# Attention scores by key differences for half of the key pairs, in a convolution and attention kernel on one core

## The reference

```python
B, C, H, W = x.shape                      # 2, 64, 96, 96
h = group_norm1(x, n1_g, n1_b)
f = dwconv(h, w3, b3) + dwconv(h, w5, b5) + dwconv(h, w7, b7)
g = jax.nn.sigmoid(conv1x1(f, gate_w, gate_b))
x = x + conv1x1(f * g, proj_w, proj_b)
h = group_norm1(x, n2_g, n2_b)
N = H * W                                 # 9216
q = conv1x1(h, q_w, q_b).reshape(B, C, N).transpose(0, 2, 1)
k = conv1x1(h, k_w, k_b).reshape(B, C, N)
v = conv1x1(h, v_w, v_b).reshape(B, C, N).transpose(0, 2, 1)
attn = jax.nn.softmax(jnp.einsum('bnc,bcm->bnm', q, k) * C ** -0.5, axis=-1)
out = jnp.einsum('bnm,bmc->bnc', attn, v)
return x + out.transpose(0, 2, 1).reshape(B, C, H, W)
```

## Time and profile before

| | |
|---|---|
| median of 3 runs | 2752.18 us (2750.35 to 2754.17) |
| the profiled execution | 2755.12 us, of which the profile's span is 2753.1 us |
| granted TensorE clock, mean over the span | 0.995 of 2.4 GHz |
| busy share of the span | PE 96%, POOL 83%, ACT 80%, DVE 68%, weight loads 41% |
| accumulating DMAs into accD | 612 of 512 KB, 4.9 us from issue to landing |
| the chain of work that ended last | 83% of it on PE |

### The profile page before, as it was taken

How to read it: one execution, slowest core, us unless ns; L and a number is a source line. 1 busy time by engine, 2 the same in 40 slices (tenths; PEclk the granted TensorE clock), 3 DMA queues, 4 the chain that set the end, 5 groups by cost and what they waited for, 6 DMA issues and landing times.

```text
span 2753.1 us, 87253 instructions
## 1 busy us (share of the span) xinstructions
PE 2650.6 (96%) x36712; PEld 1124.0 (41%) x36712; DVE 1859.0 (68%) x1942; ACT 2193.4 (80%) x2216; POOL 2298.6 (83%) x2088
## 2 busy tenths in 40 slices
PE   7889999999999999999988999999999999999998
PEld 4243344444444444444433344444444444444443
DVE  5576666767676766766557666667667666666664
ACT  4467788888888888888866788888888888888887
POOL 1356999988999898999964799999999899999987
PEclk9999999999999999999999999999999999999999
DMA  6138888877878777777601687787777777777771
GB/s 205 45 78 184 165 167 168 164 160 161 168 163 166 161 163 162 163 163 161 134 8 37 141 165 162 158 169 159 163 163 161 160 163 163 161 162 163 162 157 30
DMA packets 138706, 406.85 MB, mean 148 GB/s; under 512 B 19272, under 2 KB 45384, under 8 KB 137808
## 3 DMA queue, kind: packets, MB, share of 16 engines
q0 software_dynamic: 102816, 356.56, 64.3%
q1 hardware_dynamic: 35504, 44.75, 6.0%
HBM read 16.41 MB, written 9.44 MB: 9 GB/s over the span
## 4 chain that ended last, share of the span: by engine, by line
PE 83%; DVE 8%; issue 3%; POOL 2%; ACT 2%; DMA 1%; SPq 0%; ACTq 0%; POOLq 0%; DVEq 0%
PE ps L1053 36%; PE ps L1042 32%; PE ps L1062 9%; DVE mxp L838 5%; POOL arena L493 2%; PE ps L1187 2%; DVE ot L888 2%; ACT arena L597 1%; PE ps L1102 1%; DVE pvc L875 1%; DMA accD<-arena 1%; PE ps L1215 1%; ACT ps L633 1%; PE ps L1090 1%; PE ps L1230 0%
## 5 line engine op out<-in xcount | busy, mean ns | idle before, releaser
L838 DVE TENSOR_REDUCE mxp<-ps 128x1 f32<-128x1024 f32 x1296 | 1581.6, 1224 | 742.7 <-PE ps L1062 742.6
L493 POOL TENSOR_TENSOR arena<-arena 128x512 f32<-128x512 f32 x1224 | 1746.2, 1427 | 184.2 <-ACT arena L597 99.3
L597 ACT ACTIVATE arena<-ps,bnd 128x1024 f32<-128x1024 f32 x1296 | 1373.7, 1111 | 340.2 <-PE ps L1042 317.4
L1053 PE MATMUL ps<-arena,vals 64*64 64x512 f32 x10368 | 1243.2, 591 | 6.6 <-DVE pvc L875 6.6
L1042 PE MATMUL ps<-arena 64*64 64x512 f16 x15552 | 1064.7, 376 | 10.6 <-ACT ps L633 7.3
L633 ACT ACTIVATE ps<-arena 128x1024 f32<-128x1024 f16 x612 | 628.7, 1027 | 54.2 <-ACT arena L597 1.5
L1042 PEld LDWEIGHTS ps<-arena 64*64 64x64 f16 x15552 | 456.5, 106 | 432.1 <-issue 152.3
L1062 PE MATMUL ps<-arena,QM 64*64 64x512 f16 x5184 | 514.5, 385 | 37.5 <-DVE mxp L838 32.5
L1053 PEld LDWEIGHTS ps<-arena,vals 64*64 64x64 f32 x10368 | 368.8, 133 | 408.2 <-issue 319.3
L510 POOL DMA_DIRECT2D accD<-arena x544 | 488.6, 898 | 13.2 <-DMA accD<-arena 9.9
L1062 PEld LDWEIGHTS ps<-arena,QM 64*64 64x64 f16 x5184 | 150.4, 103 | 547.1 <-DVE mxp L838 480.1
(11 more groups left out here) (127 smaller groups left out, 707.2 us busy)
## 6 DMA issues: line engine op xcount, KB each, us to landing
accD<-arena POOLq DMA_DIRECT2D x612, 512.0 KB, 4.9
accD<-accD POOLq DMA_DIRECT2D x34, 512.0 KB, 7.1
arena<-accD POOLq DMA_DIRECT2D x68, 256.0 KB, 5.2
arena<-arena SPq DMA_DIRECT2D x144, 64.0 KB, 2.5
arena<-in_x_rows SPq DMA_DIRECT2D x8, 816.0 KB, 9.8
xs<-in_x SPq DMA_DIRECT2D x4, 1152.0 KB, 16.0
f_scratch<-arena SPq DMA_DIRECT2D x32, 144.0 KB
f<-f_scratch SPq DMA_DIRECT2D x16, 288.0 KB, 10.6
```

Of the source, the lines that this page charges most:

```text
L493: nc.gpsimd.tensor_tensor(accA[:, n % 2, :], accA[:, n % 2, :], e, ALU.add).then_inc(adda_free, 1)
L597: nc.scalar.activation(E[:, :, slot_of(n % 2, p), :], ps[:, S_BANK + 2 * buf:S_BANK + 2 * buf + 2, :], ACT.Exp, scale=bnd[:, 6:7]).then_in ...
L838: nc.vector.reduce_max(flat(mxp[:])[:, v:v + 1], flat(ps[:, bank:bank + 2, :]), AX.X).then_inc(mx_free, 1)
L1053: a = nc.tensor.matmul(ps[C * t:C * t + C, ACC_BANK + r, :], V[rows, p, t, :], E[rows, t, slot_of(par, p), :], start=(p == 0), stop=(p == ...
```

## The change

Keys of a chunk of 512 are now split: for pairs with p % 4 of 2 or 3, the key matrix holds the difference to the keys of the pair two before (`KD` its high part, the second half of KL its low part). Their matmuls add onto the scores that already stand in the buffer, so such a pair has neither a seed nor the `one16` product: 12 matmuls, and the maximum is already subtracted. Pairs with p % 4 of 0 or 1 are seeded, both, from pair 4 on. In blocks other than the first of an image, pair 24 is not seeded (the row sums of the block before use its banks), and pairs 0 and 1 never are. E has 10 slots instead of 12. GpSimd adds two pairs at a time (128 x 1024). ScalarE copies both banks of weighted values (128 x 1024) and a DMA folds them; VectorE's `add_pv` goes. GpSimd adds the output's two terms (`finish`) after ScalarE added a bias to one of them (`add_bias`); VectorE's `write_out` goes from the blocks. The next block's maxima are placed before the last exponential of a block instead of after it, by 16 matmuls instead of 8. SP loads the second image's x and convolved values in pieces over the first image's blocks.

```diff
-NSLOT = 12
+NSLOT = 10
...
-        def is_seeded(b, p):
-
-            return b in SEEDED and p % 2 == 1 and p >= 3
+        def by_difference(p):
+
+            return p % GP >= 2
+
+        def is_seeded(j, p):
+
+            return p >= GP and not by_difference(p) and not (j and p == RESTART)
...
-                nc.gpsimd.tensor_tensor(accA[:, n % 2, :], accA[:, n % 2, :], e, ALU.add).then_inc(adda_free, 1)
+                at = slot_of(n, 2 * g)
+                pool.wait_ge(e_ready, NPAIR * n + 2 * g + 3)
+                pool.wait_ge(adda_free, NSLOT + NPAIR * n + 2 * g)
+                nc.gpsimd.tensor_tensor(accA[:, n % 2, :], accA[:, n % 2, :], E[:, 0, at:at + 2, :].rearrange("p s c -> p (s c)"),
+                                        ALU.add).then_inc(adda_free, 2)
...
+                def keys_and_difference(c, chunk):
+
+                    n = 2 * NCH * b + c
+                    cols = slice(chunk * CH, chunk * CH + DIFF)
+                    pool.wait_ge(t_ready, n + 1)
+                    pool.wait_ge(hi_ready, n + 1)
+                    nc.gpsimd.tensor_tensor(T[:, c % 4, DIFF:CH], T[:, c % 4, DIFF:CH], T[:, c % 4, 0:DIFF], ALU.subtract
+                                            ).then_inc(diff_ready, 1)
+                    nc.gpsimd.tensor_tensor(KL[:, cols], T[:, c % 4, 0:DIFF], KH[:, cols], ALU.subtract)
...
-                nc.scalar.activation(flat(pvc[:]), ps[:, ACC_BANK, :], ACT.Copy).then_inc(acc_copied, 1)
+                nc.scalar.activation(pvc.rearrange("p r h c -> p r (h c)"), ps[:, ACC_BANK:ACC_BANK + 2, :], ACT.Copy
+                                     ).then_inc(acc_copied, 1)
+
+            def add_bias(b, j):
+
+                done = (b * (NBLK // 2) + j // 2) * 32
+                act.wait_ge(xst_ready[j % 2], done + 32)
+                nc.scalar.activation(xst[:, j % 2, :], xst[:, j % 2, :], ACT.Identity, bias=prm[:, VB:VB + 1]
+                                     ).then_inc(xst_biased, 1)
...
                 for p in range(NPAIR):
+                    if p == NPAIR - 1 and j + 1 < NBLK:
+                        place_maxima(n + 1)
                     exponentials(n, p)
-                    if p == ROW_SUMS + 3 and j:
+                    if p == RESTART - 1 and j:
                         copy_row_sums(n - 1, S_BANK)
-                    if p + 2 < NPAIR and is_seeded(b, p + 2):
+                    if p + 2 < NPAIR and is_seeded(j, p + 2):
                         seed(b, j, p + 2)
                     if p == 1 and j:
                         move_pv(n - 1)
+                    if p == RESTART + 2 and j:
+                        add_bias(b, j - 1)
...
-                terms = ((KH[:, keys], 0), (KL[:, keys], 0), (KH[:, keys], 1), (one16[:], 2))
-                if seeds is not None:
-                    pe.wait_ge(seeded, seeds)
+                if is_seeded(j, p):
+                    pe.wait_ge(seeded, seeds_before(b, j, p + 1))
+                keys = slice(p * P, (p + 1) * P)
+                of_hi, hi = KH, keys
+                if by_difference(p):
+                    at = p // GP * DIFF + p % 2 * P
+                    of_hi, hi = KD, slice(at, at + P)
+                terms = ((of_hi[:, hi], 0), (KL[:, keys], 0), (of_hi[:, hi], 1), (one16[:], 2))
+                opens = not by_difference(p) and not is_seeded(j, p)
+                if not opens:
                     terms = terms[:3]
```

More of the change, by code:

```diff
@@ L437, in _ @@
                 if b + 1 < B:
-                    load_x(b + 1)
+                    load_x_chunk(b + 1, 0)
                     sp.wait_ge(v_ps, NCH * (b + 1))
[L440 to L444, removed]
+                    for i in range(1, NCH - 1):
+                        attend(b, i, 0, True)
+                        load_x_chunk(b + 1, i)
+                        attend(b, i, 1, True)
+                        get_convolved(b + 1, (i - 1) // 2, ((i - 1) % 2,))
+                else:
+                    with sp.Fori(1, NCH - 1) as ii:
+                        for par in (0, 1):
+                            attend(b, ii, par, True)
                 attend(b, NCH - 1, 0, True, max_queries=False)
+                if b + 1 < B:
+                    load_x_chunk(b + 1, NCH - 1)
+                    get_convolved(b + 1, NSET - 1, (1,))
                 attend(b, NCH - 1, 1, True, queries=False, max_queries=False)
@@ L712, in _ @@
                         n = 2 * NCH * b + i
+                        before = ITEMS[i - 1]
                         by, plus = bnd[:, 4 + which:5 + which], bnd[:, 7 + which:8 + which]
@@ L720, in _ @@
                                              bias=plus, scale=by).then_inc(t_ready, 1)
+                        if i and before[0] == 1:
+                            act.wait_ge(diff_ready, NCH * b + before[1] + 1)
+                            nc.scalar.activation(KD[:, before[1] * DIFF:(before[1] + 1) * DIFF], T[:, (i - 1) % 4, DIFF:CH], ACT.Copy
+                                                 ).then_inc(dh_ready, 1)
                 place_maxima(blk(b, 0))
@@ L1124, in visit, with following @@
                         max_scores(par, v // NCH, v % NCH, NVIS * (n + 2) + v)
+                def following(p):
+                    q = p + 2
+                    if q < NPAIR:
+                        if q == RESTART and not first:
+                            pe.wait_ge(rs_copied, n)
+                        scores(b, j, q, n0 + p + 1)
+                    elif looks:
+                        if q == NPAIR:
+                            pe.wait_ge(m_ready, n + 2)
+                            pe.wait_ge(qs_in[1 - par], staged)
+                        scores(b, j + 1, q - NPAIR, n0 + p + 1)
+                if looks:
+                    pe.wait_ge(qm_in[1 - par], max_staged)
                 for p in range(0, NPAIR, 2):
-                    if p == 0 and looks:
-                        pe.wait_ge(qm_in[1 - par], max_staged)
                     if p == NPAIR - AHEAD and looks == 2:
```

246 lines of the change are left out of this document (140 added, 106 removed).

## The result

The changed kernel takes 2930.18 us (median of 4 executions, 2927.93 to 2930.86), the kernel before 2752.22 (also of 4, 2750.35 to 2754.17): ratio 1.0645, 95% interval 1.0627 to 1.0664. It is 6.5% slower. The profiled execution took 2930.86 us, with a span of 2929.1.

A forecast was written before the change was run, and what follows sets the result against it. TensorE was taken to set the pace, with ScalarE's seeds nearly as long a path. 2755.1 + 223 (36 blocks at +6.2) - 9.5 (loads) + 5 (prologue) = 2973.6, forecast as 2970 us, 7.9% slower; range 2900 to 3040.

The forecast's parts named there:

- The closed loop: TensorE's scores wait for ScalarE's second seed, delaying the next difference scores: four pairs take 8.29 instead of 7.34 us.
- Seed to seed, 2.25: ScalarE, from seed p+2's start to seed p+3's, one exponential between: 2.25 us, from 3.26 less 1.01.
- The rest of a block, 10.5 - 1.4: A block's two iterations outside the eight groups, 10.5 us before, change by -1.4 in sum.
- the maxima's spread, +0.2: 16 small matmuls instead of 8 when maxima are spread: +0.2 us a block, bounds 0 and 0.4.
- The loads' -9.5: Spreading the second image's loads saves the second block's extra 9.5 us.
- VectorE's two lines: Output write L888 and sum L875 leave the chain: 1.5 us a block saved, bounds 0 and 2.5.
- The prologues: More GpSimd operations and a further ScalarE copy in the prologue, mostly under VectorE's reductions: +5 us, from 0 to +20.
- Waits at scores p+3: TensorE idle before the second seeded pair's scores, 1.2 to 1.5 us, eight or so a block, some 400 us in all.
- A: Rival: faster, the second seed does not hold TensorE (wait under about 0.6 us a group); 2670 or 2570 us; 7%.
- B: Rival: much slower, TensorE's clock falls after each standstill, 430 us more, 3400 us; 3%.
- C: Rival: slower still, a dear wide GpSimd sum makes exponentials wait for slots; 3080 us, from 3050 to 3120; 7%.
- D: Rival: seed delays and TensorE's saving cancel, at a wait near 0.6 us; 2%.

The follow-up runs named there:

- experiment 5: Changed kernel with seeds at p % 4 = 3 and 0, the even pair weighed between the scores in most iterations, `add_bias` two pairs later: 2726.58 us.
- experiment 2: Changed kernel with the even pair's weighing and second look-ahead between the two scores in iterations whose pairs are both seeded: 2671.90 us, 0.9707 of the kernel before.
- experiment 8: Changed kernel with an unread 256-element ScalarE copy in front of the first seed of a group (p % 4 = 2), 7 a block forecast: 2951.81 us.

## Why the prediction was right, and where its sizes were off

**The closed loop** is shown. Its length follows TensorE's part of it (2.79 and 1.72 us, in experiment 5, give 8.22 and 7.14) and ScalarE's (0.10 and 0.30 more give 8.32 and 8.52), and ScalarE's work outside it costs nothing. The changed kernel itself has a third length of TensorE's part: in the last block of an image no look-aheads stand in it, it is 2.36, and the group is 7.78 (from seed-held scores to the next):

```profile
2881.33 0.84 PE L1131 MATMUL ps<-arena 64*64 64x512 f16 x12 [1.31 <-ACT ps L720]
...
2883.69 0.41 PE L1131 MATMUL ps<-arena,KD 64*64 64x512 f16 x4
...
2889.11 0.84 PE L1131 MATMUL ps<-arena 64*64 64x512 f16 x12 [1.31 <-ACT ps L720]
```

With one seed a group in the other blocks, or with TensorE's part at 1.74 (experiment 2), it no longer holds TensorE.

**Seed to seed, 2.25: too long.** It is 2.15. I took the two exponentials of the earlier trace rows less one and kept 1.20 for the one that is left; a single exponential between two seeds starts 0.07 before the seed's end and takes 1.10. My lower bound (2.16) was the right reading. The loop was 8.29 on paper and 8.22 on the chip: 0.07 x 8 = 0.56 us a block.

**The rest of a block, 10.5 - 1.4: a little too dear.** With 8 x 8.22 taken off 74.26, 8.5 is left where I had 9.1. The bias cost 0.39, not 0.5. And the maxima's spread, +0.2 in the forecast, is negative: in the kernel before, the 8 matmuls of 128 columns took 0.35 us (1006.54 to 1006.89), the 16 of 64 columns take 0.12, as TensorE's rows show, before and after:

```profile
1006.54 0.41 PE L1071 MATMUL ps<-ident,negm 128*64 128x128 f16 x8
1006.89 1.09 PE L1053 MATMUL ps<-arena,vals 64*64 64x512 f32 x8
```

```profile
985.52 0.29 PE L1162 MATMUL ps<-ident,negm 64*64 64x64 f16 x16
985.64 1.06 PE L1142 MATMUL ps<-arena,vals 64*64 64x512 f32 x8
```

Together 0.54 of the 0.6. Two more terms can be read from the starts of the difference scores over the changed kernel's block:

```profile
990.62 0.39 PE L1131 MATMUL ps<-arena,KD 64*64 64x512 f16 x4
...
998.89 0.41 PE L1131 MATMUL ps<-arena,KD 64*64 64x512 f16 x4
...
1031.75 0.41 PE L1131 MATMUL ps<-arena,KD 64*64 64x512 f16 x4
...
1037.47 0.83 PE L1131 MATMUL ps<-arena 64*64 64x512 f16 x12
...
1040.29 0.39 PE L1131 MATMUL ps<-arena,KD 64*64 64x512 f16 x4
```

The first group, with `move_pv`, takes 8.27, 0.05 over the others and not 0.2. The group of pairs 22 to 25, with the row sums, takes 8.54, and 8.29 + 1.01 - 0.8 = 8.50 was forecast; that they agree is luck. I had put the row sums into a wait for a seed, but pair 24 has no seed, and the scores of pair 25 (1037.47) wait for none. The terms for VectorE's two lines were not measured apart.

**The sum.** 36 x (6.2 - 5.06) = 41 us, and the forecast was 40 too high. The loads' -9.5 held (-9.6). The prologues cost 1 us, not 5: the first exponential of the first image comes 0.55 later (166.76 against 166.21), that of the second, counted from the last copy of the first image, 0.47 later (77.42 us against 76.95). Against that the last blocks of the two images became 6.8 and 6.6 us longer (71.14 from 64.33, 67.61 from 61.06), 3 us in sum more than two times 5.06 and 1 us more than the 6.2 each that I had taken for them: they have no look-aheads, and TensorE waits longer for the seeds there (1.31 a group).

**What was to be seen.** Waits at scores p+3, ended by the seed line: 257 of 0.99 on average, 253 us, not some 290 of 1.4, so shorter than the 1.2 to 1.5 that I had asked for. By starts TensorE is held 1.07 us (1019.02 + 0.65 to 1020.74), of which the profile counts 0.91 as idle. The look-ahead in the group waits for VectorE (1016.85, 0.23 later than I put it), so TensorE comes 0.23 later and waits the less; the loop's length does not change by that. There are 7 such waits in most blocks, since the group of pairs 22 to 25 has none. PE is busy 89%, not 85%. The groups were to be 8.2 to 8.4 apart, the second block like the others: so it is.

**The rivals.** A asked for a wait under 0.6 us; it is about 1. GpSimd's wide sum is indeed cheap, 2.35 us undisturbed and 2.40 on average, against 3.00 for the two of the earlier trace rows:

```profile
L523 POOL TENSOR_TENSOR arena<-arena 128x1024 f32<-128x1024 f32 x576 | 1381.2, 2398 | 390.4 <-ACT arena L673 338.2
```

By the Trainium skill, "GPSIMD Engine Reference", section 3.1, my estimate was 2.2; the undisturbed 2.35 is 7% above it, and the page's rate was a better guide than the row. It gained nothing, since GpSimd is off the path. B: the granted clock is 0.996 with 0.9 us of idle in every 8.2. (Its price had a slip: half of 3.4 us is 1.7, which gives 490 us and not 430.) The swing that the Trainium skill describes in "TensorE: Matmul & The Clock Gate", section "A second HAM failure mode: psum-queue depth-cycling", does not show in this trace. C: exponentials waited for DMA 1.7 us in all, so 10 slots are enough. D would have needed a wait near 0.6.

## What to carry to other kernels

When two engines hand buffers to each other, write down the cycle (what each step waits for, until the first step can start again) and add its parts; the busy shares can all fall while that sum grows. What stands in the cycle between the last handing over and the first is as much its length as the waits are: moving 1.05 us of independent matmuls out of that stretch gave back 258 us. Look at the order of every engine in it: an experiment that put the seeds into different iterations of TensorE left them neighbours on ScalarE.

## What the runs showed of the hardware that was not expected

On ScalarE a row's length is not what an instruction costs the next one. Where the next waits for nothing of it, it starts before the row's end: 0.30 after the start of a copy shown as 0.41, 0.96 after that of a seed shown as 1.03. Where it must wait for the end, it starts 0.09 to 0.10 after it. So a seed behind the exponential whose banks it overwrites comes 0.19 later than the copy in experiment 8 did, and there is room for a small independent instruction: the same copy cost 0.10 us in front of the seed and 0.30 behind it.

From the first one's start to the start of the next matmul, sixteen matmuls of 64 columns took 0.12 us where eight of 128 took 0.35, though the columns are the same in sum. The two differ in rows and tile as well (128*64 before, 64*64 after), and no run tells which of these it is.
